# A mixer block with an expert layer: first layer as f32 on array quadrants, and second and first layer alternated unit by unit

## The chip, the cores and the metric

One core of one Trainium2 chip. The time is the device time of a launch in microseconds. TensorE (PE) multiplies into PSUM; ScalarE (ACT) does the GELUs and many copies, VectorE (DVE) and GpSimd (POOL) the elementwise work, and SyncE (SP) issues the transfers.

## The reference

Four images of 64 x 64 pixels and 16 channels, in f32. First a frequency block with a residual (a cosine transform, windowed attention and convolutions, the inverse transform), then a mixture of experts over tokens. `_ln_c` and `_ln_t` are layer norms.

```python
x = x + _L0_conv_ref(_ln_c(x), ...)         # transform, attention, 1x1 / 3x3 / 1x1 convolutions, inverse transform
t = _to_tokens(x)                           # 4 images x 16 channels x 64 = 4096 tokens of 64 features
t = t + _L0_ffn_ref(_ln_t(t), ...)
# _L0_ffn_ref, 8 experts, the two best of each token, exact GELU:
weights = top_p / top_p.sum(axis=-1, keepdims=True)
xe = xn[None, :, :] * ln_g[:, None, :] + ln_b[:, None, :]
h = gelu(einsum('end,edh->enh', xe, W1) + b1[:, None, :])     # 64 -> 256
y = einsum('enh,ehd->end', h, W2) + b2[:, None, :]            # 256 -> 64
out = (weights[:, :, None] * sel).sum(axis=1)
```

## The kernel before

Images are handled in two **pairs**; the two images of a pair lie on partitions 0 to 63 and 64 to 127. Everything stays in SBUF. PSUM is four slots of 1024 f32 columns, `slot(p, n)`, each of two banks of 512. Every engine has its own program, and semaphores join them. In which order an engine goes through its stages is a table of numbers, `TURN`, one for each pair; `in_turn` sorts the stages by it. The **experts** are rounds in the same order, with the turns 80, 90, 100, ... of `round_turn(r)` for r = -2, -1, 0, ...

All eight experts are computed for all tokens, and the results are weighted with gates that are zero but for two. A **unit** u is one expert for one half of a pair (512 token columns of each of the two images): 4 halves x 8 experts = 32 units. A unit has
- `up(u)`, the first layer (L675 to L697): four tiles, k = 0, 1 (128 hidden features) times image b = 0, 1. Tokens and weights are split into a high and a low f16 part that lie on the two halves of the partitions; a tile is two parts times two column halves, thus four f16 matmuls with all 128 rows and 64 columns of the array (form 128*64), and it fills one bank, `h_bank(n)`;
- `gelu_hidden(u)` on ScalarE (L852 to L862), one ACTIVATE of 512 columns for a tile, into `hid_of[u % 4]`;
- `down(u)`, the second layer (L699 to L712): four f32 matmuls of the form 128*64 into a bank `y_bank(u)`, of which there are two;
- `add_expert(u)` on VectorE (L1147 to L1165), which multiplies by the gate and adds to `x1`.

The rounds go two units by two: down(2r), down(2r+1), up(2r+4), up(2r+5), as AHEAD is 2. The units 0 to 3 come before the gates are there; for them only `slot(0, 1)` is free, so that its two banks take turns (`h_early`). Later six banks do (`h_late`).

What makes the f16 parts: `norm_tokens` (VectorE) leaves normed tokens, `high_part` (ScalarE, L818) rounds them to f16, `low_part` (GpSimd, L922) takes the difference, `features` (TensorE, L638) transposes both, `keep_tokens` (ScalarE, L830) copies them to `tok`. `weights_of_first` (GpSimd, L928) scales W1 and splits it.

How the gates come about: `router` (TensorE, L661), L1091 and `route` (VectorE), `tanh_gap` (ScalarE, L836), `shares` (VectorE), `gates_to_rows` (TensorE, L670), `keep_gates` (ScalarE, L840), then a store to memory and loads that spread each gate over 64 partitions (SyncE, `store_gates`, `load_gates`).

Of the kernel before, what the change touches and what calls it, by code (L numbers as in the profile page):

```python
# [53 lines left out]
    "mix_branches": (16, 18), "inverse_over_kw": (36, 41), "high_part": (29, 92), "tokens": (37, 43),  # L54
    "residual": (19, 22), "norm_tokens": (21, 24), "keep_tokens": (30, 93), "features": (42, 92), "low_part": (6, 7),
# [33 lines left out]
def constants():  # L89
# [30 lines left out]
    return out, np.eye(P, dtype=np.float16)  # L120
# [38 lines left out]
def metaformer(nc, x, small, W1, W1T, ln_b, W2, const32, const16, out):  # L159
    ctx = ExitStack()  # L160
    with ctx:
# [10 lines left out]
        def slot(p, n):  # L172

            return SLOT[2 * p + n]
# [24 lines left out]
        c16 = sb("c16", [P, P], F16)  # L199
# [6 lines left out]
        ident16 = c16[:, 0:P]  # L206
# [18 lines left out]
        w1s = sb("w1s", [P, 2, E, HID], F16)  # L225
# [8 lines left out]
        tok = sb("tok", [P, PAIRS, 2, B2, TT // 2 * P], F16)  # L234
# [21 lines left out]
        parts = [x_conv[p].bitcast(F16) for p in range(PAIRS)]  # L256
# [20 lines left out]
        def h_bank(n):  # L277

            early = EARLY * TILES
            return h_early[n % len(h_early)] if n < early else h_late[n % len(h_late)]  # L280
# [9 lines left out]
        hid = sb("hid", [P, 2, TILES, CHUNK])  # L290
        hid_of = [hid[:, 0], hid[:, 1]] + [w[:, :, :].rearrange("p (t a) n -> p t (a n)", t=TILES) for w in (w1f, w1g)]
# [6 lines left out]

        def part_of(p, part, j):

            return parts[p].rearrange("p (t a h) -> p t a h", a=2, h=H)[:, j * K:(j + 1) * K, part, :]

        def shifted(p, b, tap):
# [6 lines left out]
        const_in, const16_in, weights_in = sem("const_in"), sem("const16_in"), sem("weights_in")  # L310
# [20 lines left out]
         high_ready, parts_ready, wr_centred_ready, logits_read, tok_ready, gap_ready, tanh_ready, gparts_ready, gates_ready, coef_ready) = (sem(n) for n in (  # L331
# [3 lines left out]
             "high_ready parts_ready wr_centred_ready logits_read tok_ready gap_ready tanh_ready gparts_ready gates_ready coef_ready").split())  # L335
# [10 lines left out]
        def _(sp):  # L346
# [6 lines left out]
            sp.dma_start(c16[:, :], const16).then_inc(const16_in, 16)  # L353
# [54 lines left out]
        def _(pe):  # L408
# [229 lines left out]
            def features(p):  # L638

                pe.wait_ge(const16_in, 16)  # L640
                pe.wait_ge(logits_read, p + 1)
                to = slot(p, 1).bitcast(F16)
                for j in range(TT):
                    if j % 4 == 0:
                        pe.wait_ge(parts_ready, 2 * p + j // 4 + 1)
                    for b in range(B2):
                        a = (j // 4 * 2 + b) * CHUNK + j % 4 * P
                        mm = pe.transpose(to[:, a:a + P], parts[p][:, (j * 2 + b) * P:(j * 2 + b + 1) * P], ident16)
                    if j % 4 == 3:
                        mm.then_inc(tok_done, 1)  # L650
# [24 lines left out]
            def up(u):  # L675
# [22 lines left out]

            def down(u):  # L699
# [7 lines left out]
                for k in range(KT):  # L707
                    pe.wait_ge(gelu_ready, TILES * u + B2 * (k + 1))
# [22 lines left out]
        def _(act):  # L731
# [86 lines left out]
            def high_part(p):  # L818
                for j in range(2):
                    act.wait_ge(xn_ready, 2 * p + j + 1)  # L820
                    act.copy(part_of(p, 0, j), split(bank(xc[p], j), H)).then_inc(high_ready, 1)  # L821

# [7 lines left out]
            def keep_tokens(p):  # L830
                for j in range(2):
                    act.wait_ge(tok_done, 2 * p + j + 1)
                    act.copy(tok[:, p, j, :, :].rearrange("p b n -> p (b n)"),
                             slot(p, 1).bitcast(F16)[:, j * N:(j + 1) * N]).then_inc(tok_ready, 1)
# [17 lines left out]
            def gelu_hidden(u):  # L852
# [4 lines left out]
                for t in range(TILES):  # L857
                    k = t // B2
                    n = TILES * u + t
                    act.wait_ge(w1_done, n + 1)  # L860
                    act.activation(hid_of[u % 4][:, t, :], h_bank(n), ACT.Gelu,  # L861
# [3 lines left out]
                      keep_y, keep_yt, keep_back, keep_half, square_tokens, high_part, keep_tokens, tanh_gap, keep_gates)  # L865
# [5 lines left out]
        def _(pool):  # L871
# [50 lines left out]
            def low_part(p):  # L922

# [268 lines left out]
```

## Time and profile before

| | us |
|---|---|
| median of 3 runs | 228.63 |
| the runs | 228.62 to 231.39 |
| span of the profiled execution, first to last instruction | 227.4 |
| TensorE busy | 206.7 |
| ScalarE busy | 128.1 |
| VectorE busy | 123.8 |
| GpSimd busy | 47.0 |

The profiled execution has no time of its own on record beside its span; the median of the runs is 1.2 us above it, which is what lies before the first and after the last instruction. Busy times are of one execution. A matmul of f32 operands leaves two records in the trace, one of f16 operands one; the records of one engine overlap, so that a group's busy time divided by its records is less than the mean length of one. The form 128*64 behind a matmul is the rows and columns of the array that it uses, and four matmuls of the form 64*64 can lie on four different quadrants.

### The profile page before, as it was taken

The numbers are of one execution on the slowest core, as the hardware profiler recorded it, in microseconds if no ns is written. First come the engines' busy times: TensorE is split into PE (matmuls) and PEld (weight loads), VectorE is DVE, ScalarE is ACT, GpSimd is POOL, SyncE is SP. The second block draws the span as 40 slices with busy tenths as digits, with TensorE's granted clock in tenths as the row PEclk, the third lists the DMA queues.
The fourth block names the chain that finished last, engine by engine and source line by source line (L and its number), as shares of the span: only waits on it lengthen the run. The fifth ranks groups of instructions, "written<-read, shape, count | busy, mean of one in ns | idle before, by whom it ended". The sixth has DMA issues, their size and how long they took to land.

```text
span 227.4 us, 4913 instructions
## 1 busy us (share of the span) xinstructions
PE 206.7 (91%) x2096; PEld 113.6 (50%) x2096; DVE 123.8 (54%) x232; ACT 128.1 (56%) x207; POOL 47.0 (21%) x50
## 2 busy tenths in 40 slices
PE   7699788999976898988899799999999999999993
PEld 3395667566334577963524244444444444444430
DVE  0582055659949977999731633554334553334555
ACT  2256942035338553669685387666786666786640
POOL 5560393040069992030400000000000000000000
PEclk9979999999999999999699999999999999999998
DMA  6990000000000000000005953260804508063001
GB/s 219 294 265 14 0 3 6 3 0 7 0 0 4 0 3 0 3 0 0 3 0 164 220 128 69 82 151 0 184 3 108 122 4 184 0 150 84 0 0 46
DMA packets 6596, 14.35 MB, mean 63 GB/s; under 512 B 2736, under 2 KB 4144, under 8 KB 5680
## 3 DMA queue, kind: packets, MB, share of 16 engines
q1 hardware_dynamic: 6576, 14.06, 24.7%
q8 instruction: 16, 0.26, 0.5%
q14 instruction: 4, 0.03, 0.0%
HBM read 12.87 MB, written 1.18 MB: 62 GB/s over the span
## 4 chain that ended last, share of the span: by engine, by line
PE 68%; ACT 9%; DMA 7%; POOL 6%; DVE 6%; SPq 1%; issue 1%; POOLq 1%; DVEq 0%
PE psum L710 22%; PE psum L694 21%; PE psum L538 7%; DMA xs<-in_x 3%; DMA wide<-gate_store 2%; PE psum L512 2%; POOL place L920 2%; ACT place L747 2%; PE psum L634 2%; PE psum L548 2%; PE psum L424 2%; POOL place L926 2%; ACT hid L861 1%; POOL place L919 1%; PE psum L557 1%
## 5 line engine op out<-in xcount | busy, mean ns | idle before, releaser
L694 PE MATMUL psum<-tok,w1s 128*64 128x512 f16 x512 | 60.8, 383 | 1.3 <-ACT hid L861 0.8
L1160 DVE SCALAR_TENSOR_TENSOR term<-psum,sm,wide 128x512 f32<-128x512 f32 x32 | 24.0, 750 | 62.1 <-PE psum L710 51.6
L861 ACT ACTIVATE hid<-psum,b1p 128x512 f32<-128x512 f32 x64 | 38.2, 701 | 16.7 <-PE psum L694 16.3
L694 PEld LDWEIGHTS psum<-tok,w1s 128*64 128x64 f16 x512 | 28.7, 110 | 35.9 <-issue 9.1
L861 ACT ACTIVATE w1f<-psum,b1p 128x512 f32<-128x512 f32 x32 | 19.6, 688 | 17.1 <-PE psum L694 17.0
L710 PE MATMUL psum<-hid,w 128*64 128x512 f32 x128 | 28.9, 593 | 0.0
L1165 DVE TENSOR_TENSOR x<-x,term 128x512 f32<-128x512 f32 x32 | 22.1, 692 | 1.1
L861 ACT ACTIVATE w1g<-psum,b1p 128x512 f32<-128x512 f32 x32 | 19.7, 714 | 0.2
L710 PEld LDWEIGHTS psum<-hid,w 128*64 128x64 f32 x128 | 9.1, 137 | 15.1 <-issue 9.4
L710 PE MATMUL psum<-w1g,w 128*64 128x512 f32 x64 | 15.1, 594 | 1.4 <-DVE term L1160 1.4
L538 PE MATMUL psum<-h_pad,tap_bd 64*64 64x512 f32 x144 | 15.9, 589 | 0.0
L710 PE MATMUL psum<-w1f,w 128*64 128x512 f32 x64 | 15.1, 594 | 0.1
L777 ACT ACTIVATE place<-psum 128x512 f32<-128x512 f32 x4 | 2.2, 594 | 15.4 <-PE psum L538 15.4
L538 PEld LDWEIGHTS psum<-h_pad,tap_bd 64*64 64x64 f32 x144 | 6.8, 133 | 7.5 <-issue 7.5
L911 POOL TENSOR_TENSOR place<-place 128x1024 f32<-128x1024 f32 x2 | 4.7, 2353 | 26.0 <-ACT place L777 26.0
L710 PEld LDWEIGHTS psum<-w1g,w 128*64 128x64 f32 x64 | 4.5, 137 | 10.9 <-issue 6.6
L414 PE MATMUL psum<-still 128*128 128x512 f16 x28 | 8.0, 435 | 1.3 <-POOL still L872 1.3
L926 POOL TENSOR_TENSOR place<-place 128x512 f16<-128x512 f32 x4 | 4.6, 1166 | 19.7 <-ACT place L821 19.7
L998 DVE TENSOR_TENSOR wide<-psum,sm 128x1024 f32<-128x1024 f32 x4 | 4.7, 1220 | 7.0 <-PE psum L498 7.0
L735 ACT ACTIVATE place<-psum 128x512 f32<-128x512 f32 x4 | 2.4, 597 | 10.3 <-PE psum L424 10.3
L710 PEld LDWEIGHTS psum<-w1f,w 128*64 128x64 f32 x64 | 4.5, 137 | 6.7 <-issue 3.1
L992 DVE TENSOR_TENSOR wide<-psum,c 128x512 f32<-128x512 f32 x4 | 2.6, 682 | 9.6 <-PE psum L486 9.6
(147 smaller groups left out, 295.4 us busy)
## 6 DMA issues: line engine op xcount, KB each, us to landing
wide<-gate_store SPq DMA_DIRECT2D x14, 512.0 KB, 6.4
xs<-in_x SPq DMA_DIRECT2D x2, 512.0 KB, 5.6
w1f<-in_W SPq DMA_DIRECT2D x2, 512.0 KB, 10.0
block_out<-x SPq DMA_DIRECT2D x4, 256.0 KB, 6.4
wide<-gate_store SPq DMA_DIRECT2D x2, 384.0 KB, 5.1
c<-const SPq DMA_DIRECT2D x1, 548.5 KB, 4.4
hid<-in_W1T SPq DMA_DIRECT2D x1, 512.0 KB, 10.3
w<-in_W SPq DMA_DIRECT2D x1, 512.0 KB, 11.8
```

The source lines that it names most:

```text
L414: pe.matmul(where, still[:, 0:P], still[:, 0:where.shape[1]], start=True, stop=True)
L424: mm = pe.matmul(slot(p, 0)[:, cp * P:(cp + 1) * P], xs[:, p, cp * P:(cp + 1) * P], dct_h, start=True, stop=True)
L512: mm = pe.matmul(bank(slot(p, 0), swapped)[rows_of(crossed(half, swapped)), 0:side], const("pick")[rows_of(half), first:first + H], column ...
L538: mm = pe.matmul(bank(slot(p, 0), b)[rows_of(crossed(half, b)), :], tap_bd[rows_of(half), tap, :], shifted(p, b, tap)[rows_of(half)], star ...
L694: mm = pe.matmul(h_bank(n)[side * H:(side + 1) * H, :], w1s[:, part, e, k * P + side * H:k * P + (side + 1) * H], tok[:, pair, half, b, :] ...
L710: mm = pe.matmul(y_bank(u)[b * H:(b + 1) * H, :], w2[:, e * KT + k, :], hid_of[u % 4][:, B2 * k + b, :], start=k == 0, stop=k == KT - 1)
L861: act.activation(hid_of[u % 4][:, t, :], h_bank(n), ACT.Gelu, bias=b1p[:, e * KT + k:e * KT + k + 1]).then_inc(gelu_ready, 1)
L911: pool.tensor_tensor(x_conv[p], x_conv[p], xd[p], ALU.add).then_inc(xconv_ready, 1)
L926: pool.tensor_tensor(part_of(p, 1, j), split(bank(xc[p], j), H), part_of(p, 0, j), ALU.subtract).then_inc(parts_ready, 1)
L998: dve.tensor_tensor(prod[p].rearrange("p (s o q) n -> p o s q n", s=2, o=2)[:, j], slot(p, j).rearrange("p (s q n) -> p s q n", s=2, n=P), ...
L1160: dve.scalar_tensor_tensor(term[:, u % 2, :], y_bank(u), b2t[:, e:e + 1], gate_b[part][:, e % (E // 2), :], ALU.add, ALU.mult).then_inc(te ...
L1165: dve.tensor_tensor(x1p, x1p, term[:, u % 2, :], ALU.add).then_inc(add_done, 1)
```

## The change

- Tokens stay f32: `high_part`, `low_part`, the f16 constant and its transfer, and the two f16 steps of `weights_of_first` go. `features` transposes eight blocks in f32, where there were sixteen in f16, and `keep_tokens` copies 2 x 512 columns for a pair.
- `up(u)`: two steps k. A step is four f32 matmuls with 64 rows and 64 columns of the array, image b on the rows of its partitions, one for each quadrant, and fills both banks of a slot, `h_slot(n)`, bank b with image b.
- GELUs are two for a unit, of 1024 columns.
- The early place is one slot, the late ones are three; both y banks lie in `slot(0, 0)`. A third hidden buffer in `hid` replaces the one over `w1g`, which now holds the weights in use.
- The rounds alternate: down(2r), up(2r+4), down(2r+1), up(2r+5).

```diff
-        h_early = [bank(slot(0, 1), 0), bank(slot(0, 1), 1)]
-        h_late = h_early + [bank(slot(1, 1), 0), bank(slot(1, 1), 1), bank(slot(1, 0), 1), bank(slot(0, 0), 0)]
-        y_banks = [bank(slot(0, 0), 1), bank(slot(1, 0), 0)]
+        h_early = [slot(0, 1)]
+        h_late = h_early + [slot(1, 1), slot(1, 0)]
+        y_banks = [bank(slot(0, 0), 1), bank(slot(0, 0), 0)]
...
             def features(p):
...
-                pe.wait_ge(const16_in, 16)
                 pe.wait_ge(logits_read, p + 1)
-                to = slot(p, 1).bitcast(F16)
                 for j in range(TT):
                     if j % 4 == 0:
-                        pe.wait_ge(parts_ready, 2 * p + j // 4 + 1)
-                    for b in range(B2):
-                        a = (j // 4 * 2 + b) * CHUNK + j % 4 * P
-                        mm = pe.transpose(to[:, a:a + P], parts[p][:, (j * 2 + b) * P:(j * 2 + b + 1) * P], ident16)
+                        pe.wait_ge(xn_ready, 2 * p + j // 4 + 1)
+                    mm = pe.transpose(slot(p, 1)[:, j * P:(j + 1) * P], xc[p][:, j * P:(j + 1) * P], ident)
...
-                for t in range(TILES):
-                    k, b = divmod(t, B2)
-                    n = TILES * u + t
-                    before = last_in(h_bank, n)
+                moving = bank(tok[:, pair, :], half)
+                for k in range(KT):
+                    n = KT * u + k
+                    before = last_in(h_slot, n)
                     if before >= 0:
                         pe.wait_ge(gelu_ready, before + 1)
-                    for part in range(2):
-                        for side in range(2):
-                            mm = pe.matmul(h_bank(n)[side * H:(side + 1) * H, :],
-                                           w1s[:, part, e, k * P + side * H:k * P + (side + 1) * H], tok[:, pair, half, b, :],
-                                           start=part == 0, stop=part == 1)
+                    for swapped in range(2):
+                        for b in range(B2):
+                            side = crossed(b, swapped)
+                            mm = pe.matmul(bank(h_slot(n), b)[rows_of(side), :],
+                                           w1g[rows_of(b), e, k * P + side * H:k * P + (side + 1) * H], moving[rows_of(b), :],
+                                           start=True, stop=True)
                     mm.then_inc(w1_done, 1)
...
             def experts(r):
...
-                if r >= 0:
-                    down(2 * r)
-                    down(2 * r + 1)
-                for u in (2 * (r + AHEAD), 2 * (r + AHEAD) + 1):
-                    if u < UNITS:
-                        up(u)
+                for odd in range(2):
+                    if r >= 0:
+                        down(2 * r + odd)
+                    if 2 * (r + AHEAD) + odd < UNITS:
+                        up(2 * (r + AHEAD) + odd)
...
-                for t in range(TILES):
-                    k = t // B2
-                    n = TILES * u + t
+                for k in range(KT):
+                    n = KT * u + k
                     act.wait_ge(w1_done, n + 1)
-                    act.activation(hid_of[u % 4][:, t, :], h_bank(n), ACT.Gelu,
+                    act.activation(hid_of[u % 4][:, B2 * k:B2 * (k + 1), :].rearrange("p b n -> p (b n)"), h_slot(n), ACT.Gelu,
                                    bias=b1p[:, e * KT + k:e * KT + k + 1]).then_inc(gelu_ready, 1)
...
-            def low_part(p):
-
-                for j in range(2):
-                    pool.wait_ge(high_ready, 2 * p + j + 1)
-                    pool.tensor_tensor(part_of(p, 1, j), split(bank(xc[p], j), H), part_of(p, 0, j), ALU.subtract).then_inc(parts_ready, 1)
...
-                link(pool.tensor_tensor(w1g[:, :, :], w1f[:, :, :], lng.unsqueeze(2).broadcast_to([P, E, HID]), ALU.mult))
-                link(pool.tensor_copy(w1s[:, 0, :, :], w1g[:, :, :]))
-                pool.tensor_tensor(w1s[:, 1, :, :], w1g[:, :, :], w1s[:, 0, :, :], ALU.subtract).then_inc(w1_ready, 1)
+                pool.tensor_tensor(w1g[:, :, :], w1f[:, :, :], lng.unsqueeze(2).broadcast_to([P, E, HID]), ALU.mult).then_inc(w1_ready, 1)
```

TensorE between the first transposed tokens and the first downs. Before, L648 is `features`, L634 `tokens` of pair 1, L694 `up`, L666 `router`, L673 `gates_to_rows`, L710 `down`:

```order
L648 MATMUL psum<-c,place 128x128 x16
L634 MATMUL psum<-c,x 128x128 x8
L694 MATMUL psum<-tok,w1s 64x512 x32
L666 MATMUL psum<-wr_centred,x 128x16 x8
L648 MATMUL psum<-c,place 128x128 x16
L694 MATMUL psum<-tok,w1s 64x512 x32
L673 MATMUL psum<-c,gates 128x128 x2
L710 MATMUL psum<-hid,w 64x512 x8
```

After, where L635 is `features`, L625 `tokens`, L682 `up`, L653 `router`, L660 `gates_to_rows`, L698 `down`:

```order
L635 MATMUL psum<-c,place 128x128 x8
L625 MATMUL psum<-c,x 128x128 x8
L682 MATMUL psum<-tok,w1g 64x512 x16
L653 MATMUL psum<-wr_centred,x 128x16 x8
L635 MATMUL psum<-c,place 128x128 x8
L682 MATMUL psum<-tok,w1g 64x512 x16
L660 MATMUL psum<-c,gates 128x128 x2
L698 MATMUL psum<-hid,w 64x512 x4
```

The stages keep their order; `features` and `up` have half as many matmuls.

TensorE from the first downs on, before and then after:

```order
L710 MATMUL psum<-hid,w 64x512 x8
L694 MATMUL psum<-tok,w1s 64x512 x32
L710 MATMUL psum<-w1f,w 64x512 x4
L710 MATMUL psum<-w1g,w 64x512 x4
L694 MATMUL psum<-tok,w1s 64x512 x32
L710 MATMUL psum<-hid,w 64x512 x8
```

```order
L698 MATMUL psum<-hid,w 64x512 x4
L682 MATMUL psum<-tok,w1g 64x512 x8
L698 MATMUL psum<-hid,w 64x512 x4
L682 MATMUL psum<-tok,w1g 64x512 x8
L698 MATMUL psum<-hid,w 64x512 x4
L682 MATMUL psum<-tok,w1g 64x512 x8
L698 MATMUL psum<-w1f,w 64x512 x4
L682 MATMUL psum<-tok,w1g 64x512 x8
L698 MATMUL psum<-hid,w 64x512 x4
```

A down of four matmuls and an up of eight now follow each other singly, where eight of L710 and thirty-two of L694 did.

ScalarE from the first f16 part to the gates. Before, L821 is `high_part`, L833 `keep_tokens`, L816 `square_tokens`, L861 the GELUs, L838 `tanh_gap`, L843 `keep_gates`:

```order
L821 CAST place<-place 128x8x64 x2
L833 COPY tok<-psum 128x1024 x2
L816 ACTIVATE place<-psum 128x512 x2
L861 ACTIVATE hid<-psum,b1p 128x512 x8
L838 ACTIVATE st<-st 128x16
L821 CAST place<-place 128x8x64 x2
L833 COPY tok<-psum 128x1024 x2
L838 ACTIVATE st<-st 128x16
L861 ACTIVATE w1f<-psum,b1p 128x512 x4
L861 ACTIVATE w1g<-psum,b1p 128x512 x4
L843 COPY gate_rows<-psum 128x128 x2
```

After, L815 is `keep_tokens`, L803 `square_tokens`, L841 the GELUs, L819 `tanh_gap`, L824 `keep_gates`:

```order
L815 COPY tok<-psum 128x512 x2
L803 ACTIVATE place<-psum 128x512 x2
L841 ACTIVATE hid<-psum,b1p 128x1024 x4
L819 ACTIVATE st<-st 128x16
L815 COPY tok<-psum 128x512 x2
L819 ACTIVATE st<-st 128x16
L841 ACTIVATE hid<-psum,b1p 128x1024 x2
L841 ACTIVATE w1f<-psum,b1p 128x1024 x2
L824 COPY gate_rows<-psum 128x128 x2
```

The casts are gone, four GELUs of 1024 stand for eight of 512, and the order is otherwise the same.

## Rows read from the trace of the kernel before

**Rows 1.** The page, busy us, share of the span and instructions.

```profile
PE 206.7 (91%) x2096; PEld 113.6 (50%) x2096; DVE 123.8 (54%) x232; ACT 128.1 (56%) x207; POOL 47.0 (21%) x50
```

**Rows 2.** Busy time by window; columns: window, length, engines (instructions), granted clock, DMA.

```profile
130.00:150.00 20.00, 20.00 (x144) 8.84 (x142) 8.27 (x12) 14.21 (x24) 0.00 (x0) 1.00 0.47 107
```

**Rows 3.** The chain that ended last, regular part: start us, us, what.

```profile
130.54 3.45 PE psum L694 x32
133.99 3.43 PE psum L710 x16
```

**Rows 4.** The same chain, 102 to 130 us.

```profile
102.37 0.66 ACT hid L861
...
103.07 0.64 PE psum L694 x4
...
103.73 0.70 ACT hid L861
...
113.07 0.59 ACT w1f L861
...
118.48 0.18 ACT gate_rows L843 x2
118.66 1.53 DMA gate_store<-gate_rows
...
127.80 0.76 DVE term L1160
...
128.60 1.94 PE psum L710 x8
```

**Rows 5.** The same chain, the 3x3 convolution of pair 0.

```profile
39.17 7.73 PE psum L538 x70
```

**Rows 6.** Groups by form: busy us, mean ns of one, idle before.

```profile
L861 ACT ACTIVATE hid<-psum,b1p 128x512 f32<-128x512 f32 x64 | 38.2, 701 | 16.7 <-PE psum L694 16.3
L710 PE MATMUL psum<-hid,w 128*64 128x512 f32 x128 | 28.9, 593 | 0.0
...
L998 DVE TENSOR_TENSOR wide<-psum,sm 128x1024 f32<-128x1024 f32 x4 | 4.7, 1220 | 7.0 <-PE psum L498 7.0
...
L833 ACT COPY tok<-psum 128x1024 f16<-128x1024 f16 x4 | 4.0, 1012 | 3.4 <-PE psum L648 3.3
...
L992 DVE TENSOR_TENSOR wide<-psum,c 128x512 f32<-128x512 f32 x4 | 2.6, 682 | 9.6 <-PE psum L486 9.6
...
L811 ACT COPY place<-psum 128x512 f32<-128x512 f32 x4 | 2.3, 586 | 3.4 <-PE psum L616 3.4
```

**Rows 7.** TensorE in order of time: start us, us, records; changes of form.

```profile
28.76 1.09 PE L458 MATMUL psum<-place,enter_bd 64*64 64x512 f32 x8 [0.66 <-ACT place L747]
29.77 1.14 PE L465 MATMUL psum<-place,conv_bd 128*64 128x64 f32 x16
...
48.58 1.98 PE L548 MATMUL psum<-wide,c 128*128 128x512 f32 x4
50.49 2.10 PE L512 MATMUL psum<-wide,c 64*64 64x64 f32 x128
```

**Rows 8.** All engines in order of time, around unit 0 and the route.

```profile
95.56 2.00 PE L625 MATMUL psum<-c,place 128*128 128x128 f32 x16
...
99.73 2.00 PE L634 MATMUL psum<-c,x 128*128 128x128 f32 x16
...
107.01 1.96 PE L666 MATMUL psum<-wr_centred,x 128*128 128x16 f32 x16
...
109.01 0.29 DVE L1091 TENSOR_TENSOR place<-psum,st 128x128 f32<-128x128 f32 x1 [0.86 <-PE psum L666]
...
110.15 0.81 DVE L1103 TENSOR_TENSOR place<-place,st 128x128 f32<-128x128 f32 x1
```

**Rows 9.** Two windows, columns as in rows 2.

```profile
68.00:70.00 2.00, 1.08 (x10) 0.86 (x8) 1.93 (x4) 1.19 (x4) 1.84 (x3) 1.00 0.01 4
110.00:111.00 1.00, 0.94 (x10) 0.67 (x9) 0.93 (x3) 0.15 (x1) 0.81 (x1) 0.50 0.00 0
```

More of the change, by code:

```diff
@@ L53 @@
     "inverse_over_kh": (35, 40), "keep_back": (24, 27), "keep_half": (25, 28), "square_tokens": (26, 31),
-    "mix_branches": (16, 18), "inverse_over_kw": (36, 41), "high_part": (29, 92), "tokens": (37, 43),
-    "residual": (19, 22), "norm_tokens": (21, 24), "keep_tokens": (30, 93), "features": (42, 92), "low_part": (6, 7),
+    "mix_branches": (16, 18), "inverse_over_kw": (36, 41), "tokens": (37, 43),
+    "residual": (19, 22), "norm_tokens": (21, 24), "keep_tokens": (30, 93), "features": (42, 92),
     "router": (39, 91), "route": (23, 25), "gates_to_rows": (101, 102), "shares": (26, 27), "biases": (20, 20),
@@ L119, in constants @@
     out[:, CONST["small_index"]] = np.arange(E, 0, -1)[None, :]
-    return out, np.eye(P, dtype=np.float16)
+    return out
 SMALL = {}
@@ L156, in small_weights, with metaformer @@
     return out
-def metaformer(nc, x, small, W1, W1T, ln_b, W2, const32, const16, out):
+def metaformer(nc, x, small, W1, W1T, ln_b, W2, const32, out):
     ctx = ExitStack()
@@ L233, in metaformer @@
         x1 = sb("x1", [P, PAIRS, N])
-        tok = sb("tok", [P, PAIRS, 2, B2, TT // 2 * P], F16)
+        tok = sb("tok", [P, PAIRS, N])
         still = sb("still", [P, CHUNK], F16)
@@ L255, in metaformer @@
         back = x_conv
-        parts = [x_conv[p].bitcast(F16) for p in range(PAIRS)]
         h2 = [place[4][:, p, :] for p in range(PAIRS)]
@@ L267, in metaformer, with h_slot @@
         mix = [wide[1][:, p, 0:N].rearrange("p (g n) -> p g n", n=H) for p in range(PAIRS)]
-        h_early = [bank(slot(0, 1), 0), bank(slot(0, 1), 1)]
-        h_late = h_early + [bank(slot(1, 1), 0), bank(slot(1, 1), 1), bank(slot(1, 0), 1), bank(slot(0, 0), 0)]
-        y_banks = [bank(slot(0, 0), 1), bank(slot(1, 0), 0)]
+        h_early = [slot(0, 1)]
+        h_late = h_early + [slot(1, 1), slot(1, 0)]
+        y_banks = [bank(slot(0, 0), 1), bank(slot(0, 0), 0)]
         TILES = B2 * KT
         EARLY = 2 * AHEAD
-        def h_bank(n):
-            early = EARLY * TILES
+        def h_slot(n):
+            early = EARLY * KT
             return h_early[n % len(h_early)] if n < early else h_late[n % len(h_late)]
@@ L288, in last_in @@
             return max((k for k in range(n) if which(k) is which(n)), default=-1)
-        hid = sb("hid", [P, 2, TILES, CHUNK])
-        hid_of = [hid[:, 0], hid[:, 1]] + [w[:, :, :].rearrange("p (t a) n -> p t (a n)", t=TILES) for w in (w1f, w1g)]
+        hid = sb("hid", [P, 3, TILES, CHUNK])
+        hid_of = [hid[:, 0], hid[:, 1], hid[:, 2], w1f[:, :, :].rearrange("p (t a) n -> p t (a n)", t=TILES)]
         gate_b = [wide[n][:, 0, :].rearrange("p (e n) -> p e n", n=CHUNK) for n in range(2)]
@@ L297, in metaformer @@
         gate_store = nc.dram_tensor("gate_store", (PAIRS, 2, B2, E * CHUNK), F32)
-        def part_of(p, part, j):
-            return parts[p].rearrange("p (t a h) -> p t a h", a=2, h=H)[:, j * K:(j + 1) * K, part, :]
         def shifted(p, b, tap):
@@ L330, in metaformer @@
          attn_ready, y_ready, yt_ready, mix_ready, xout_ready, back_ready, half_ready, x1_ready, csq_ready, xn_ready,
-         high_ready, parts_ready, wr_centred_ready, logits_read, tok_ready, gap_ready, tanh_ready, gparts_ready, gates_ready, coef_ready) = (sem(n) for n in (
+         wr_centred_ready, logits_read, tok_ready, gap_ready, tanh_ready, gparts_ready, gates_ready, coef_ready) = (sem(n) for n in (
              "sq_ready dh_ready dw_ready xd_ready h1_ready halo_ready xt_ready gram_ready prod_ready tk_ready "
@@ L832, in keep_tokens @@
                     act.wait_ge(tok_done, 2 * p + j + 1)
-                    act.copy(tok[:, p, j, :, :].rearrange("p b n -> p (b n)"),
-                             slot(p, 1).bitcast(F16)[:, j * N:(j + 1) * N]).then_inc(tok_ready, 1)
+                    act.copy(bank(tok[:, p, :], j), bank(slot(p, 1), j)).then_inc(tok_ready, 1)
             def tanh_gap(p):
@@ L933, in weights_of_first @@
                 pool.wait_ge(xt_ready, 1)
-                link(pool.tensor_tensor(w1g[:, :, :], w1f[:, :, :], lng.unsqueeze(2).broadcast_to([P, E, HID]), ALU.mult))
-                link(pool.tensor_copy(w1s[:, 0, :, :], w1g[:, :, :]))
-                pool.tensor_tensor(w1s[:, 1, :, :], w1g[:, :, :], w1s[:, 0, :, :], ALU.subtract).then_inc(w1_ready, 1)
-            for stage, (p,) in in_turn((weights_of_first, join, high, low_part)):
+                pool.tensor_tensor(w1g[:, :, :], w1f[:, :, :], lng.unsqueeze(2).broadcast_to([P, E, HID]), ALU.mult).then_inc(w1_ready, 1)
+            for stage, (p,) in in_turn((weights_of_first, join, high)):
                 stage(p)
@@ L1178 @@
     a = {n: np.asarray(v) for n, v in inputs.items()}
-    const32, const16 = constants()
+    const32 = constants()
     arrays = {
@@ L1184 @@
         "in_ln_b": a["L0_ffn_ln_b"].reshape(1, E * H), "in_W2": a["L0_ffn_W2"],
-        "const32": const32, "const16": const16,
+        "const32": const32,
     }
```

16 lines of the change are left out of this document (4 added, 12 removed).

## The prediction

> **What bounds the kernel now.** I read the page's busy shares first, to see which engine is a candidate: TensorE is busy for 206.7 of 227.4 us, ScalarE and VectorE for little more than half [rows 1]. Busy shares average over stages, so the windows come next: in 130 to 150 us TensorE is busy for all 20.00 us at full granted clock, and ScalarE for only 14.21 [rows 2]. In this expert stage a GELU or a VectorE operation that gets shorter is worth nothing. The chain of waits shows how regular it is: rounds of 3.45 us (two first layers) and 3.43 us (two second layers), each piece ended by TensorE itself [rows 3]. So one unit costs 1.725 + 1.715 = 3.44 us, and an edit counts if it changes that or the time at which the regular part begins.
>
> That start is set by the gates. Down(3) can begin only once VectorE has read down(1), and that waits for the gates from memory: 118.48 gates copied to rows, 118.66 store, then the loads, 127.80 VectorE, 128.60 down(3) [rows 4]. Ahead of the copy ScalarE has to finish the GELUs of units 2 and 3, which stand before it in its queue. From 102.37 to 118.48 the chain therefore alternates TensorE and ScalarE: 0.64 us of matmul, 0.70 us of GELU, with 0.02 and 0.04 between [rows 4]. That is 1.40 us for two tiles, because two banks take turns: while ScalarE reads one, TensorE fills the other.
>
> **Up on quadrants, in itself.** Before, a tile is eight records of f16 in two column halves; 32 records take 3.45 us [rows 3]. After, a step k is four f32 matmuls, each 64 rows by 64 columns of the array, on four different quadrants. The nearest row is the 3x3 convolution, L538, with the same shape and quadrants: 70 records in 7.73 us [rows 5], four records (one per quadrant) at a time, so 17.5 groups of 0.44, or 0.43 with the start taken off. An f32 matmul leaves two records, a step is two groups (0.86 us) and a unit four (1.72). Against 1.725 the gain is 0.01 us per unit, 0.3 us over the stage. If the four ran one after another the price would be four times that; the convolution excludes it, unless something in the new operands differs. Down is untouched: four groups, 1.715.
>
> **Switches between the two shapes.** This is the term that decides. Before, both layers use the form 128*64, and going from one to the other costs nothing that can be seen: two downs are eight groups, which at 0.43 are 3.44 us, and the chain has 3.43 for them, the change to the ups included [rows 3]. After, down is 128*64 and up 64*64, and they alternate unit by unit. Where the old kernel changes form I compare start to start. L458 (64*64, 512 columns, f32) is two groups, 0.86 us by the convolution's pace, and L465 (128*64) starts 1.01 us after it: 0.15 too late. L548 (128*128) has four groups, 1.72, and the 64*64 matmuls behind it start 1.91 us after it: 0.19 too late [rows 7]. So between 0.10 us (if a part of the 0.15 belongs to L458's start after idling) and 0.19; I take 0.16, near L458, whose two forms are the ones of the change. A gain is excluded, since a change of form saves no column.
>
> The Trainium skill (TensorEngine Tiling (Array Packing), Key Properties) says that changing the tiling mode, not merely the tile, drains TensorE. Read strictly, the next matmul starts when the last one has ended, 0.59 us after its start, the length of a record of L710 [rows 6], instead of 0.43; that is 0.16 per switch, and the trace's 0.15 to 0.19 agree. By that rule the kernel before pays nothing in this stage, and the sum for the new one would be 8.2 instead of 8.0 us.
>
> The number of switches that count: from down(3) on, the order is down(3), up(7), ... down(27), up(31), then four downs. Each up is entered and left once: 25 ups, 50 switches, **8.0 us** (5.0 to 9.5). Had it stayed two by two, it would be half of that.
>
> **GELUs of 1024 columns.** Half as many, longer. No row shows one. A copy of 512 from PSUM takes 0.586, of 1024 f16 elements 1.012: 0.43 for 512 more. VectorE pays 0.54 for that (0.682 to 1.220) [rows 6]. So 0.701 + 0.43 = 1.13, with 1.24 as the upper end; ScalarE is the engine in question, so 1.13. (The Trainium skill, ScalarE: Activation LUTs, What ACT_TABLE_LOAD costs, gives an estimate of 280 + 0.833 x 1024 ns = 1.13 us for a GELU with a bias operand; the sum would not move.) In the regular part this is 2.27 us per unit beside 3.75 on TensorE: covered. Three slots are enough there, since up(u) needs a slot whose GELU belongs to unit u-2 or to the first step of unit u-1, and that one began a unit's time before.
>
> **The early units, 0 to 3.** Here they are not covered. The early place was two banks in turn; it is now one slot of both banks. A step's matmuls wait for the last step's GELU and the GELU waits for them: nothing overlaps. One step by the rows: four quadrant matmuls after a wait, 1.09 (L458, the same eight records [rows 7]), + 0.02 + 1.13 + 0.04 = 2.28 us, against 1.40 for the same work before. Step by step:
> - Up to unit 0. The f16 halves (L821 on ScalarE, L926 on GpSimd) go; on TensorE features(0) waited for them and held up tokens(1), which began at 99.73 [rows 8]. Now eight f32 transposes follow L625 at about 97.5, at tokens(1)'s pace of 16 records in 1.8 us 0.11 each, so 0.9; tokens(1) runs from 98.4, unit 0 from 100.3 with the change of form, and the first GELU starts after 1.09 at 101.4 instead of 102.37: 1.0 earlier.
> - Units 0 and 1: GELUs end 3 x 2.28 + 1.13 = 7.97 us later, 109.4, instead of 107.8. The last matmuls end at 108.2 instead of 107.0, where the router's began to follow (L666 [rows 8]).
> - The router of pair 1 stands behind them on TensorE, and VectorE's route behind the router: L1091 moves from 109.01 to 110.2. One VectorE operation of the route was drawn out beside a GpSimd half (L1103, 0.81, where L1091 of the same size took 0.29 [rows 8]); without it some 0.5 us come back. ScalarE's tanh for pair 1 waits for that route and stands ahead of the GELU of unit 2, which starts at 113.5 instead of 113.07 [rows 4].
> - Units 2 and 3: again 7.97, to 121.5. Gates copied at 121.5 instead of 118.48: **3.0 later**, and so store, load and the term of unit 1, which ends at 131.6 instead of 128.56.
>
> **Unit by unit.** Before, down(2), down(3) stood together and TensorE idled 1.4 us ahead of down(3). Now up(6) lies between. From 120.7: downs 0, 1, 2, ups 4, 5, 6 and six switches are 5.1 + 5.2 + 1.0 = 11.3, so down(3) starts at 132.0, just behind the term; **3.4 later** than 128.60. In return up(6), 1.73 us, no longer lies behind it.
>
> Everything else is free: less weight preparation on GpSimd (L935, L936), whose result nobody waits for before unit 0, a 32 KB constant less behind xs in the DMA queue, and shorter copies of tokens inside the first bullet.
>
> **The sum.** +3.4 (start) - 1.7 (up(6) moved ahead) - 0.3 (pace) + 8.0 (switches) = +9.4 us. On the profiled span, 227.4 + 9.4 = 236.8; the median of the runs, 228.63, is 1.2 us above the span, which I keep: **238.0 us**, 4.1% slower.
>
> **The rivals.**
> - The clock falls among the early units. In the old trace it is granted at 0.50, the level of 1.2 GHz, from 110 to 111 us, after the router's matmuls of 16 columns and an idle stretch [rows 8, 9]. From 68 to 70 us TensorE was busy for 1.08 of 2.00 and the clock stayed at 2.4 GHz [rows 9]. The new chain keeps it busy for 1.09 of 2.28, less than that. At half clock a step's 0.86 us of columns doubles; three of the eight steps give +2.6: 240.6. Against it: the old chain, with its idle gaps, kept the full clock. Chance 0.20.
> - Not slower: the switches are hidden. If the queue prepares the other form's weights during the running matmuls and 0.15 was L458's start after idling, then +3.0 - 1.7 - 0.3 = +1.0: 229.6. The point from which it decides: 2% is 4.6 us, which is (4.6 - 1.4) / 50 = 0.064 us per switch; below it the change reads as none. L548, which did not idle, speaks against it. Chance 0.10.
> - It doesn't do what it says: the quadrants run in pairs only, for instance because each row half now writes a bank of its own. Then each up costs 1.7 more, 28 of them 48 us: about 286. L538 speaks against it. Chance 0.03.
> - Faster: the shorter way to unit 0 and a route without GpSimd beside it would have to bring the gates earlier; even a GELU of 0.6 us for 1024 columns, 8 x 0.53 = 4.2 us less, on top of hidden switches gives only 229.6 - 4.2 = 225.4. Chance 0.02.
>
> **How the numbers follow.** The forecast has the remaining 0.65. Its own bounds: switches 5.0 to 9.5 and GELU up to 1.24 (8 x 0.11 = 0.9) give 235.0 to 240.4. Down to 234 for a chain that closes better than I think, up to 242 for the clock: 234 to 242 leaves out the hidden switches, the serial quadrants, the faster case and a little of the clock case. About 2% is what a measurement here tells from no change: 233.2 is that line, so slower 0.88, same 0.10, faster 0.02.
>
> **What would show it.** In the changed profile: records of the first layer with four at a time and 0.43 between groups; start to start of an up and a down in the regular part 1.87 to 1.9 each instead of 1.72, a unit 3.75; GELUs of 1.13; the chain between 101 and 121 us made of pairs 1.09 + 1.13; gates copied near 121.5; down(3) without an idle ahead of it. Wrong would be a unit at 3.45 (no price for switches), a clock row of 0.5 between 102 and 121, or an idle of TensorE in the regular part before a slot or a y bank.

## The result, and the profile after

The median of four runs is 244.57 us (243.2 to 244.9), against 228.62 before. The ratio is 1.066, with a 95% interval of 1.060 to 1.072: 16 us slower, where 9.4 were forecast, and outside the range of 234 to 242. The profiled execution took 244.9 us; its span is 242.9.

The page of the changed kernel: busy us, the granted clock in 40 slices of 6.07 us, and two groups.

```profile
PE 218.7 (90%) x2080; PEld 99.4 (41%) x2080; DVE 122.2 (50%) x232; ACT 116.2 (48%) x139; POOL 36.4 (15%) x44
...
PEclk9999999999999999955759999999999999999999
...
L682 PE MATMUL psum<-tok,w1g 64*64 64x512 f32 x512 | 67.5, 638 | 7.4 <-ACT hid L841 6.2
L841 ACT ACTIVATE hid<-psum,b1p 128x1024 f32<-128x1024 f32 x48 | 51.2, 1112 | 43.4 <-PE psum L682 43.4
```

TensorE's share is as before [rows 1]. The slices of the clock are new: 5, 5, 7 and 5 between 103 and 128 us, where the page of the kernel before had one slice of 6 there, and one of 7 in the first 20 us. The GELU is 1.11 us long, as forecast from the copies [rows 6].

The regular part and its end, in the chain of waits, answer to [rows 3]:

```profile
226.27 1.88 PE psum L682 x16
228.15 1.87 PE psum L698 x8
...
231.90 7.04 PE psum L698 x32
```

The end of the same chain in the kernel before:

```profile
216.63 6.89 PE psum L710 x32
```

A unit takes 1.88 + 1.87 = 3.75 us, where it was 3.44. That is the forecast number. From down(3) on, at 138.27, it is 100.7 us to the end of the last down (231.90 + 7.04 = 238.94); before it was 94.9 (from 128.60 to 216.63 + 6.89 = 223.52). The forecast had +6.0 for this stretch and it is +5.8.

The way there, in the same chain, answers to [rows 4]:

```profile
100.64 1.12 ACT hid L841
...
101.80 1.13 PE psum L682 x8
102.96 1.12 ACT hid L841
...
104.13 2.03 PE psum L682 x8
...
109.33 3.54 PE psum L653 x16
...
113.24 1.97 PE psum L635 x8
...
117.19 1.12 ACT hid L841
...
123.67 1.99 PE psum L682 x8
...
126.28 2.63 PE psum L698 x8
...
138.27 1.87 PE psum L698 x8
```

The first two steps are what was forecast, 1.13 of TensorE and 1.12 of ScalarE, 0.8 us earlier than said. The third step's matmuls take 2.03 us, the router 3.54 (1.96 before [rows 8]), the transposes 1.97, down(0) 2.63. The windows give the reason:

```profile
100.00:105.00 5.00, 2.53 (x20) 0.51 (x16) 4.56 (x19) 2.41 (x3) 0.00 (x0) 0.89 0.00 0
105.00:110.00 5.00, 3.76 (x20) 1.04 (x12) 1.52 (x4) 1.72 (x2) 0.00 (x0) 0.50 0.00 0
...
140.00:160.00 20.00, 20.00 (x134) 5.51 (x136) 8.26 (x12) 10.60 (x10) 0.00 (x0) 1.00 0.40 85
```

Shorter windows say when it fell:

```profile
103.50:104.00 0.50, 0.00 (x0) 0.00 (x0) 0.42 (x3) 0.50 (x1) 0.00 (x0) 0.88 0.00 0
104.00:104.50 0.50, 0.37 (x4) 0.30 (x8) 0.43 (x3) 0.07 (x1) 0.00 (x0) 0.50 0.00 0
```

From 103.9 us on the clock is granted at 0.50, the level of 1.2 GHz. That is one of the things that the prediction named as a sign of being wrong, "a clock row of 0.5 between 102 and 121". TensorE was busy for 2.53 of 5.00 us in the window from 100 to 105, and waited on ScalarE in between for at most 1.24 us at a time. The Trainium skill (TensorE: Matmul & The Clock Gate, A second HAM failure mode: psum-queue depth-cycling) describes this: small idle times between groups of matmuls, when PSUM is cycled, make the clock go to and fro between the two levels. The trace agrees, with idle times of 1.24 us and a clock that was 1.00 again from 117.5 to 121.0 and 0.50 after it, to 127.8.

Down(3) starts at 138.27 instead of 128.60, 9.7 us later, where 3.4 were forecast. This is the miss.

### The profile page after: what moved, and what is told of

Its sections match the earlier page's. It is cut to its first block, busy times and chain, and to the rows that moved or that the text cites. A ratio compares the mean times of both kernels' runs of the same rounds, so it can differ in the third digit from the quotient of the medians.

```text
span 242.9 us, 4806 instructions
## 1 busy us (share of the span) xinstructions
PE 218.7 (90%) x2080; PEld 99.4 (41%) x2080; DVE 122.2 (50%) x232; ACT 116.2 (48%) x139; POOL 36.4 (15%) x44
## 4 chain that ended last, share of the span: by engine, by line
PE 76%; ACT 7%; DVE 7%; POOL 3%; DMA 3%; issue 1%; POOLq 1%; SPq 1%; DVEq 0%
PE psum L682 27%; PE psum L698 25%; PE psum L529 6%; DMA sm<-in_small 3%; ACT hid L841 2%; PE psum L653 2%; PE psum L503 2%; ACT place L734 2%; PE psum L539 2%; PE psum L625 2%; POOL place L899 1%; PE psum L548 1%; PE psum L635 1%; PE psum L489 1%; POOL place L898 1%
## 5 line engine op out<-in xcount | busy, mean ns | idle before, releaser
L682 PE MATMUL psum<-tok,w1g 64*64 64x512 f32 x512 | 67.5, 638 | 7.4 <-ACT hid L841 6.2
L841 ACT ACTIVATE hid<-psum,b1p 128x1024 f32<-128x1024 f32 x48 | 51.2, 1112 | 43.4 <-PE psum L682 43.4
L698 PE MATMUL psum<-hid,w 128*64 128x512 f32 x192 | 46.8, 612 | 0.0
L682 PEld LDWEIGHTS psum<-tok,w1g 64*64 64x64 f32 x512 | 16.4, 136 | 53.6 <-ACT hid L841 28.4
L698 PEld LDWEIGHTS psum<-hid,w 128*64 128x64 f32 x192 | 12.0, 138 | 32.8 <-issue 25.9
L841 ACT ACTIVATE w1f<-psum,b1p 128x1024 f32<-128x1024 f32 x16 | 17.1, 1112 | 15.4 <-PE psum L682 15.4
L698 PE MATMUL psum<-w1f,w 128*64 128x512 f32 x64 | 15.4, 603 | 0.0
L698 PEld LDWEIGHTS psum<-w1f,w 128*64 128x64 f32 x64 | 4.0, 136 | 10.8 <-issue 8.5
L900 POOL TENSOR_TENSOR place<-place 128x512 f32<-128x512 f32 x4 | 6.9, 1722 | 0.3
L899 POOL TENSOR_TENSOR place<-place,coef_rest 128x512 f32<-128x512 f32 x4 | 6.3, 1577 | 0.3
L653 PEld LDWEIGHTS psum<-wr_centred,x 128*128 128x128 f32 x32 | 5.4, 261 | 1.6 <-issue 1.6
L898 POOL TENSOR_TENSOR place<-place 128x512 f32<-128x512 f32 x4 | 5.6, 1393 | 0.4 <-ACT place L769 0.4
```

The costliest lines, as they stand in the source:

```text
L653: mm = pe.matmul(slot(p, 1)[:, j * B2 * E:(j + 1) * B2 * E], x1[:, p, j * P:(j + 1) * P], wr_centred[:, :], start=True, stop=True)
L682: mm = pe.matmul(bank(h_slot(n), b)[rows_of(side), :], w1g[rows_of(b), e, k * P + side * H:k * P + (side + 1) * H], moving[rows_of(b), :], ...
L698: mm = pe.matmul(y_bank(u)[b * H:(b + 1) * H, :], w2[:, e * KT + k, :], hid_of[u % 4][:, B2 * k + b, :], start=k == 0, stop=k == KT - 1)
L841: act.activation(hid_of[u % 4][:, B2 * k:B2 * (k + 1), :].rearrange("p b n -> p (b n)"), h_slot(n), ACT.Gelu, bias=b1p[:, e * KT + k:e * K ...
L898: link(pool.tensor_tensor(bank(h2[p], b), bank(h2[p], b), bank(x_conv[p], b), ALU.add))
L899: link(pool.tensor_tensor(bank(h2[p], b), bank(h2[p], b), coef_rest[:, :], ALU.mult))
```

## The experiments

The runs are compared by their medians; "before" was run beside each, at 229.1 or 229.2 us, and the ratios are to it. What an experiment has over the changed kernel (244.57 us) is the difference of two such medians.

### fill: TensorE kept busy while it waits

```diff
                     mm.then_inc(w1_done, 1)
+                    if u < EARLY and not (u % 2 and k):
+                        hold_clock(4, bank(slot(0, 0), 0))
```

> The changed kernel, with four idle matmuls on zeros (128x512, f16) behind six of the eight early steps, into a bank nobody reads; the work on the chain of waits is the same. My theory: the miss is the clock, granted at 0.50 for 20 us between 104 and 128. If TensorE is kept busy in the waits, the clock stays at 1.00, a step is 2.28 to 2.33 us throughout, the gates are copied near 121 instead of 126.7, and the time is 244.6 - 6 = about 238.6. Rival: the chain is long in itself (no overlap, form changes) and the clock only shows it; then the fillers change nothing or cost, 244.6 to 246.

238.31 us (237.0 to 238.96), ratio to before 1.038 (1.032 to 1.044). Two windows of it, and lines of its chain:

```profile
100.00:105.00 5.00, 4.47 (x32) 1.04 (x24) 4.55 (x19) 2.72 (x3) 0.00 (x0) 1.00 0.00 0
105.00:110.00 5.00, 4.47 (x36) 2.38 (x28) 2.02 (x6) 2.33 (x3) 0.00 (x0) 1.00 0.00 0
```

```profile
104.44 1.13 PE psum L682 x8
...
107.85 1.90 PE psum L653 x16
...
121.09 0.18 ACT gate_rows L826 x2
...
132.34 1.87 PE psum L700 x8
```

The copy of the gates in the changed kernel, in order of time:

```profile
126.74 0.43 ACT L824 COPY gate_rows<-psum 128x128 f32<-128x128 f32 x2
```

The clock is at 1.00, the router takes 1.90 us, and the gates are copied at 121.1, where the changed kernel did it at 126.7. Down(3), the last line of the chain above, starts at 132.34 instead of 138.27. The work on the chain is the same, and 6.3 us are gone with idle matmuls added. It shows in every execution: the mean granted clock over the span was 0.951 to 0.965 in the four of the changed kernel and 0.991 to 1.000 in the four of this one. This is the clock, and no other part of the change. The time is also, within 0.3, the one forecast without a fall of the clock. Two small errors offset each other in that: down(0) was 0.4 us earlier than forecast, and down(2) then waited 0.76 us for the first term, which the forecast did not have.

### two_slots: the steps overlap

```diff
-        h_early = [slot(0, 1)]
-        h_late = h_early + [slot(1, 1), slot(1, 0)]
+        h_early = [slot(0, 1), slot(0, 0)]
+        h_late = [h_early[0], slot(1, 1), slot(1, 0)]
...
+                if u == 0:
+                    pe.wait_ge(gelu_ready, EARLY * KT)
...
-                pe.transpose(slot(p, 0)[:, P:2 * P], gates[:, p].rearrange("p j b e t -> p (j b e t)"), ident).then_inc(gates_done, 1)
+                pe.transpose(slot(1, 0)[:, (1 - p) * CHUNK + P:(1 - p) * CHUNK + 2 * P], gates[:, p].rearrange("p j b e t -> p (j b e t)"), ident).then_inc(gates_done, 1)
...
-                act.copy(gate_rows[:, p, :], slot(p, 0)[:, P:2 * P]).then_inc(gates_ready, 1)
+                act.copy(gate_rows[:, p, :], slot(1, 0)[:, (1 - p) * CHUNK + P:(1 - p) * CHUNK + 2 * P]).then_inc(gates_ready, 1)
```

> The changed kernel with two early slots in turn, slot(0, 1) and slot(0, 0), so that the matmuls of a step lie beside the GELU of the last; the gates' transposes go to slot(1, 0) and down(0) waits for the last early GELU. If serial steps are the root of both the late gates and the clock: ScalarE paces at 1.12 us per step, GELUs of units 0 and 1 end near 105 and of 2 and 3 near 114.5, gates copied near 114.5 instead of 126.7, clock at 1.00, time 244.6 - 12.5 = about 232. Rival, the clock alone is what counts: about 238.6.

233.23 us (232.59 to 234.05), ratio 1.017 (1.011 to 1.024). ScalarE in order of time: pairs of GELUs, then the gates' copy:

```profile
101.42 2.12 ACT L843 ACTIVATE hid<-psum,b1p 128x1024 f32<-128x1024 f32 x2 [0.45 <-PE psum L682]
103.75 2.12 ACT L843 ACTIVATE hid<-psum,b1p 128x1024 f32<-128x1024 f32 x2 [0.20 <-PE psum L682]
...
110.54 2.10 ACT L843 ACTIVATE hid<-psum,b1p 128x1024 f32<-128x1024 f32 x2
112.84 2.12 ACT L843 ACTIVATE w1f<-psum,b1p 128x1024 f32<-128x1024 f32 x2 [0.21 <-PE psum L682]
114.86 0.42 ACT L826 COPY gate_rows<-psum 128x128 f32<-128x128 f32 x2
```

Pairs of GELUs begin 2.30 to 2.33 us apart, 1.16 per step instead of 2.28 and more. The gates are copied at 114.9 and the clock stays (mean 0.989 over the span, its one dip is in the first 20 us). Of the 11.3 us won, 6.3 are what fill won by the clock alone. The other 5.0 lie between fill, where each step still waits for the last, and this run, where it doesn't.

### two_by_two: the old order

```diff
-                for odd in range(2):
-                    if r >= 0:
-                        down(2 * r + odd)
-                    if 2 * (r + AHEAD) + odd < UNITS:
-                        up(2 * (r + AHEAD) + odd)
+                if r >= 0:
+                    down(2 * r)
+                    down(2 * r + 1)
+                for u in (2 * (r + AHEAD), 2 * (r + AHEAD) + 1):
+                    if u < UNITS:
+                        up(u)
```

> The changed kernel with the old order, two downs and then two ups. Half of the changes of form in the regular part go, 25 x 0.157 = 3.9 us; up(6) is back behind down(3), which gives back about 0.5. With a price per change of form: 241.2, a round of two units 7.18 instead of 7.49 us. Rival, the extra 0.3 us per unit belongs to the f32 quadrant matmuls themselves and not to the changes: a round stays at 7.49 and the time at 244.6 or a little more.

240.95 us (240.24 to 241.75), ratio 1.050 (1.045 to 1.056). Its chain in the regular part:

```profile
138.56 3.60 PE psum L682 x32
142.16 3.58 PE psum L698 x16
```

A round of two units is 7.18 us instead of 7.49. Two changes of form less save 0.31, thus 0.155 each. The quadrant matmuls and the rest are the same, so the rival falls. The time is within 0.3 us of the expectation.

### down_quads: no change of form

This kernel leaves out half of the second layer's sum; it only serves to time the form.

```diff
-                    for b in range(B2):
-                        mm = pe.matmul(y_bank(u)[b * H:(b + 1) * H, :], w2[:, e * KT + k, :], hid_of[u % 4][:, B2 * k + b, :],
+                    for swapped in range(2):
+                        for b in range(B2):
+                            r = crossed(b, swapped)
+                            y = bank(slot(1, 0), 1) if r else y_bank(u)
+                            mm = pe.matmul(y[rows_of(b), :], w2[rows_of(r), e * KT + k, :], hid_of[u % 4][rows_of(r), B2 * k + b, :],
```

> The changed kernel with the second layer on quadrants too: each matmul of 128 rows is two of 64 rows, and the second half of the contraction goes to a bank that nobody reads, so that half of the second layer's sum is left out. The columns on TensorE are the same, and there is no change of form among the units. Two late slots instead of three. With a price per change of form: unit 3.44 instead of 3.745, time 244.6 - 8 = 236.5. Rival, the alternation by itself or f32 on quadrants costs it: unit 3.7 or more, 244.6.

234.81 us (234.35 to 235.48), ratio 1.024 (1.018 to 1.029):

```profile
103.95 1.13 PE psum L682 x8
...
134.70 1.72 PE psum L682 x16
136.42 1.72 PE psum L701 x16
```

A unit is 1.72 + 1.72 = 3.44 us with both layers on quadrants. Alternation and f32 are the same as in the changed kernel, only the form is now one. That settles the 0.31 us per unit as the price of the two changes. What makes a change cost this, a drained array or weights loaded late, no run tells apart.

The time is 1.7 us below the expectation. From down(3) on, at 136.42, the stretch is 92.8 us instead of 100.7, the 8 us expected. Down(3) itself starts 1.85 us earlier than in the changed kernel: six changes ahead of it are gone too, and the clock fell one step later, so that the third early step took 1.13 us (at 103.95) and not 2.03.

### unit_by_unit: the new order in the kernel before

The edit of two_by_two, turned around, in the kernel before.

> The kernel before with one edit: the new order, down(2r), up(2r+4), down(2r+1), up(2r+5); the first layer stays f16 in the form 128*64. If the price lies in the change of form alone, alternation costs nothing here: a unit stays at 3.44 us, up(6) fills the 1.4 us that TensorE idles ahead of down(3), and the time is 228.7 - 1.5 = about 227.2. Rival, alternation as such costs 0.15 us each time: 25 units more with two changes, half of which there were: about +4, 232.

227.23 us (226.96 to 228.03), ratio 0.993 (0.990 to 0.995): faster by 0.7%, clear of the noise and below 2%. Its chain, from the gates' copy on (L694 is up, L710 down, as before):

```profile
117.65 0.18 ACT gate_rows L842 x2
...
128.41 1.94 PE psum L710 x8
130.34 1.73 PE psum L694 x16
132.07 1.72 PE psum L710 x8
133.79 1.73 PE psum L694 x16
```

Down(3) starts at 128.41, with up(6) before it, where the kernel before started it at 128.60 without. This execution was 1.5 us ahead of the one of the kernel before already at the convolution of pair 1 (54.02 for 55.54) and 0.8 at the gates' copy (117.65 for 118.48), so the gain is read from the medians and not from these two times. The pieces keep 1.72 and 1.73 us. Alternation costs nothing where both layers have one form.

### gelu_512: how long a GELU may be

```diff
-                    act.activation(hid_of[u % 4][:, B2 * k:B2 * (k + 1), :].rearrange("p b n -> p (b n)"), h_slot(n), ACT.Gelu,
-                                   bias=b1p[:, e * KT + k:e * KT + k + 1]).then_inc(gelu_ready, 1)
+                    for b in range(B2):
+                        ins = act.activation(hid_of[u % 4][:, B2 * k + b, :], bank(h_slot(n), b), ACT.Gelu,
+                                             bias=b1p[:, e * KT + k:e * KT + k + 1])
+                    ins.then_inc(gelu_ready, 1)
```

> two_slots with two GELUs of 512 columns for a step instead of one of 1024. In the regular part ScalarE has 2.8 us of work per unit beside 3.75 on TensorE: nothing. In the early units a step is 1.40 instead of 1.12: 1.1 us for units 2 and 3, while for units 0 and 1 the route of pair 0 on VectorE ends later anyway: 233.2 + 1.1 = 234.3. Rival, the length of a GELU is covered throughout: 233.2.

232.43 us (231.8 to 233.55), ratio 1.015 (1.012 to 1.018); two_slots had 1.017 (1.011 to 1.024), so no difference is shown; expected were 1.1 us more. ScalarE in order of time:

```profile
99.93 4.89 ACT L844 ACTIVATE hid<-psum,b1p 128x512 f32<-128x512 f32 x8 [0.45 <-PE psum L682]
...
109.66 2.42 ACT L844 ACTIVATE hid<-psum,b1p 128x512 f32<-128x512 f32 x4 [0.53 <-PE psum L682]
```

Eight GELUs take 4.89 us, 0.61 each, where one that waits for its matmul takes 0.70 [rows 4]. The four steps of units 0 and 1 are thus 4.89 us long, where two_slots has 4.45 (101.42 to 105.87). My 1.40 took the length of a single one twice. The Trainium skill (ScalarE: Activation LUTs, What ACT_TABLE_LOAD costs) has the rule, that back-to-back ACTIVATEs overlap by some 93 ns, and the trace agrees: 0.70 - 0.61 = 0.09. GELUs of 1024 are worth 0.11 us per early step, and in the time nothing that can be seen.

### f16_slots: the kernel before with slots and long GELUs

The f16 first layer writes both images' banks of a slot; slots as in two_slots, GELUs of 1024, order unit by unit.

```diff
-                for t in range(TILES):
-                    k, b = divmod(t, B2)
-                    n = TILES * u + t
+                for k in range(KT):
+                    n = KT * u + k
...
-                    for part in range(2):
-                        for side in range(2):
+                    for b in range(B2):
+                        for part in range(2):
+                            for side in range(2):
```

> The kernel before with what the experiments speak for: f16 first layer in the form 128*64, unit by unit, GELUs of 1024 columns, and two early slots of two banks in turn. ScalarE needs 1.12 us for a step of the early units instead of 1.40, so four steps of units 2 and 3 take 1.1 less, and the route starts up to 0.8 earlier: gates 1.7 earlier than before, and up(6) in the gap 1.4 to 1.7: 225.4. Rival, the gates are bound by the route and the f16 halves and not by GELUs: about 227, no better than unit_by_unit.

226.77 us (226.32 to 226.89), ratio 0.989 (0.987 to 0.992). ScalarE in order of time, units 2 and 3:

```profile
111.80 1.11 ACT L861 ACTIVATE w1f<-psum,b1p 128x1024 f32<-128x1024 f32 x1 [0.35 <-PE psum L694]
113.43 1.11 ACT L861 ACTIVATE w1f<-psum,b1p 128x1024 f32<-128x1024 f32 x1 [0.52 <-PE psum L694]
114.44 2.37 ACT L861 ACTIVATE w1g<-psum,b1p 128x1024 f32<-128x1024 f32 x2
116.71 0.42 ACT L844 COPY gate_rows<-psum 128x128 f32<-128x128 f32 x2
```

The gates come at 116.7, 0.9 us before unit_by_unit's 117.65, where the expectation had 1.7 beyond that run. The first GELUs of unit 2 are 1.63 us apart: the matmuls of the two steps ahead of the second take 3.50 us on the chain, at a clock of 0.50 from 110 to 113 us, behind the router. The expectation was 1.4 too low, and its rival (about 227) is the nearer. The run is 0.2% better than unit_by_unit, and their intervals overlap, so no difference is shown.

### all_quads, quads_tail, quads_ends: both layers on quadrants, complete

Three runs, told in this order. The second half of each contraction goes to two more y banks, and VectorE takes both halves in. In quads_tail units 28 to 31, and in quads_ends units 0 and 1 as well, have plain downs.

```diff
+                            y = bank(slot(1, 0), u % 2) if r else y_bank(u)
...
+                for r in range(2):
+                    y = bank(slot(1, 0), u % 2) if r else y_bank(u)
+                    if r:
+                        dve.tensor_tensor(term[:, r, :], y, gate_b[part][:, e % (E // 2), :], ALU.mult).then_inc(term_done, 1)
...
+        PLAIN = (0, 1, 28, 29, 30, 31)
```

**all_quads**

> two_slots with the second layer on quadrants too, and complete: the second half of each contraction goes to banks of its own, and VectorE multiplies and adds both halves (four operations per unit, 2.9 us, instead of two). No change of form among the units: 233.2 - 50 x 0.157 = 225.4, plus 1.4 for two more VectorE operations behind the last down and 0.4 for down(0), which now waits for the copied gates: 227.2. Rival, VectorE at 2.9 of 3.44 us or the y banks hold TensorE up: a unit over 3.5 us, 229 or more.

229.13 us (227.7 to 230.28), ratio 1.000 (0.997 to 1.002): 2 us more than expected. The end of its chain:

```profile
212.50 1.76 PE psum L703 x16
...
214.28 0.76 DVE term L1143
...
217.00 0.75 DVE term L1143
```

The regular part is at 3.44 as said, with VectorE busy for 15.84 of 20.00 us. But the last four downs stand together, and only the first of them is on the chain: from 214.28 on VectorE is the bound, 2.7 us per unit, four times, to 225.2. I had counted two more VectorE operations at the end, where there were eight, of which TensorE's downs cover a part.

**quads_tail**

> all_quads, but the last four downs, which follow one another, are back in the form 128*64 with one term on VectorE each. In all_quads TensorE's last down but three ends at 214.3 and VectorE needs 4 x 2.7 us for what is left, to 225.2. With plain downs there it ends at 214.3 + 0.16 (one change of form) + 5.1 + 1.5 = 221.0: 229.1 - 4.2 = about 225. Rival, the time of all_quads went elsewhere (two chains of VectorE at the first gates, regular part): 228 to 229.

224.98 us (224.07 to 225.97), ratio 0.983 (0.980 to 0.985):

```profile
209.82 1.72 PE psum L687 x16
211.54 7.04 PE psum L706 x32
...
218.60 0.76 DVE term L1153
```

The four plain downs take 7.04 us and VectorE follows at once. 4.1 us are won, 4.2 expected.

**quads_ends**

> quads_tail, and the downs 0 and 1 plain too. Down(3) waited in all_quads for both terms of unit 1, two VectorE chains of 1.4 us; one less lets it start up to 1.3 us earlier, against three or four more changes of form, 0.5 to 0.6 us: 224.3 to 225. Rival, the load of the gates bounds it all the same: no difference to quads_tail.

224.25 us, ratio 0.978 (0.975 to 0.981). Five of the six executions lie between 223.5 and 225.28, and one took 227.52; the ratio goes by the five. On its chain the downs and ups from down(0) on follow one another without a wait for the gates. The intervals of quads_tail and quads_ends overlap (0.980 and 0.981 at the near ends), so the last 0.7 us are not settled. Both beat the kernel before, by some 2%, and the changed one by 8%.

## Why the prediction was wrong

**What held.** The term that was to decide did so and had its size: 50 changes of form at 0.16 us. The stretch from down(3) on gives (5.8 + 1.7 + 0.3) / 50 = 0.156, two_by_two 0.155, down_quads 0.31 for two, which is 0.155. Quadrants run four at a time at the pace of the convolution [rows 5]; GELUs are 1.11 us; up(6) left the stretch behind down(3), and TensorE had no idle time in the regular part. The serial early step was forecast at 2.28 and is 1.13 + 1.12 + 0.06 = 2.31.

**The step that failed** is the first term of the sum, "+3.4 (start)": down(3) began 9.7 us later than before. The term counts every early step at 2.28 us, the clock at 1.00 throughout. The fall of the clock stood among the rivals, "The clock falls among the early units", with a chance of 0.20 and a price of three steps, +2.6; it happened and cost 6.3 (fill). Two things were wrong in that rival.
- The chance. "Against it: the old chain, with its idle gaps, kept the full clock" is not so, and it compared chains that differ in just this. The old chain's clock was at 0.50 from 109.8 to 113.2 us, one of two such stretches in that trace, as the row of 110 to 111 us in the same rival says. And in its early steps the old chain has 1.20 us of matmul records in 1.40 us, the new one 1.09 in 2.3. Whether the new one would fall could not be read from the old trace: the row of 68 to 70 us, with 1.08 of 2.00 us busy, kept the full clock [rows 9].
- The price. Only steps were counted. At half clock everything on the chain is longer: two steps before the router (+0.9 each), the router (3.54 instead of 1.90 at full clock), the transposes of pair 1 (about +0.9), a first step of unit 2 that now ends after the tanh and holds up its GELU, two more steps, and down(0) (2.63 for 1.94). Gates were copied at 126.7 instead of 121.5, and down(3) began 6.3 us after the forecast.

**Smaller terms.** The changed kernel reached the convolution of pair 1 0.65 us earlier than before (54.89 instead of 55.54); its clock was at 1.00 in the first 20 us, where before it was at 0.91. That depends on the execution: two_slots has the same slice of 7 on its page. What lies around the span is 2.0 us in this execution and 1.7 to 2.6 in the experiments. The 1.2 that I kept came from one execution's span and another one's time, and left 0.8 us out. It is not what lies around the kernel before either: that is 2.2 to 2.6 us in all its later executions, so the profiled one will have taken near 229.8 us (an estimate, 227.4 + 2.4).

**The sum again**, for the profiled execution: 6.3 (start of down(3)) - 0.2 (regular part and end) + 0.8 (around the span) = 6.9, and 238.0 + 6.9 = 244.9. So the clock is all but the whole of the miss.

**The parts of the change**, told apart by the runs. The form 64*64 beside 128*64 costs 8 us through the changes and nothing in itself (down_quads); one early slot costs 5.0 by waiting and 6.3 by the clock that the waiting brings down; unit by unit gains about 1.8 us in the kernel before (unit_by_unit). Tokens in f32 save the halves, which brings unit 0 forward by a good microsecond (from the convolution of pair 1 to the first GELU it is 45.75 us in the changed kernel, 46.83 in the kernel before and 46.84 in unit_by_unit, which has the halves too). No run has this edit alone.

## What to carry to other kernels

Count how often TensorE changes between forms of the array (128*64, 64*64, 128*128) in a loop, not just how many columns each form streams: 0.16 us a time is nothing once and 8 us in fifty alternations. When a double-buffered pair becomes one larger buffer, price the chain it leaves at both levels of the clock, with every piece of TensorE's work on it, the small ones too. A loop with one form throughout can pay for an extra pass on an engine with room (VectorE here), but not at the end, where nothing covers it.

## What the runs showed of the hardware

- A change between the forms 128*64 and 64*64 costs 0.155 to 0.156 us, in either direction alike (up 1.88 and down 1.87 us, both 1.72 without it), while TensorE is busy for 20.00 of 20.00 us.
- TensorE's clock fell from 1.00 to 0.50 in a stretch (100 to 105 us) where the engine never waited more than 1.24 us at once but was busy for only half the time, 2.53 of 5.00 us. It stayed there for 13.6 us, came back for 3.5 us and fell again for 6.8. Matmuls on zeros in the waits kept it at 1.00, with TensorE busy for 4.47 of 5.00 us (fill).
- A GELU of 512 columns takes 0.70 us alone and 0.61 in a row of eight; one of 1024 takes 1.11 alone, and two in a row 2.12.
